# A gated delta-rule scan in chunks: where the matmuls of the values' half and of the u half of the state update stand on TensorE

## What is computed

```python
# H, N = 4, 64 (heads, channels per head); x is (2, 4096, 256), run() goes over all tokens
def step(S, inp):
    rt, dt, kt, vt, at, bt = inp
    sa = jnp.einsum('bhij,bhj->bhi', S, at)
    S = S * dt[:, :, None, :] + sa[..., None] * bt[:, :, None, :] + vt[..., None] * kt[:, :, None, :]
    y = jnp.einsum('bhij,bhj->bhi', S, rt)
    return (S, y)
...
xn = _layernorm(x, axis=-1)
s = _L0_attn_ref(xn, ...)        # token mixing, projections, the scan, group norm, output projection
g = _silu(_L0_ffn_ref(xn, L0_ffn_w_gate, L0_ffn_w_up, L0_ffn_w_down))
x = x + s * g
```

## Time and profile before

| | |
|---|---|
| median of 3 runs | 1603.26 us (1598.4 to 1605.24) |
| the profiled execution | 1603.78 us, of which 1602.3 us lie between its first and last instruction |
| PE busy | 1493.2 us (93%) |
| DVE busy | 1261.4 us (79%) |
| ACT busy | 1073.9 us (67%) |
| POOL busy | 335.8 us (21%) |
| mean granted TensorE clock | 0.982 of full speed |
| chain that ended last | PE 85%, DVE 6%, issue 2%, DMA 2%, ACT 2% |

### The profile page before, as it was taken

How to read it: one execution, slowest core, us unless ns; L and a number is a source line. 1 busy time by engine, 2 the same in 40 slices (tenths; PEclk the granted TensorE clock), 3 DMA queues, 4 the chain that set the end, 5 groups by cost and what they waited for, 6 DMA issues and landing times.

```text
span 1602.3 us, 56437 instructions
## 1 busy us (share of the span) xinstructions
PE 1493.2 (93%) x24384; PEld 1028.5 (64%) x24384; DVE 1261.4 (79%) x2661; ACT 1073.9 (67%) x1889; POOL 335.8 (21%) x362
## 2 busy tenths in 40 slices
PE   3579999999999999899999989999999999999977
PEld 1256767576676767667676666757666675766755
DVE  2788888888888888788887878888888888878623
ACT  3658587585858758576775858768585876858412
POOL 3020301313040131302213030131304013130101
PEclk9799999999999999999999999999999999999979
DMA  4011120301112030110302112030111203011110
GB/s 149 14 21 21 35 47 17 62 19 40 28 35 47 17 62 19 33 34 24 58 16 46 35 21 47 17 62 19 40 36 32 42 17 62 20 40 28 34 34 28
DMA packets 251462, 58.37 MB, mean 36 GB/s; under 512 B 223696, under 2 KB 250704, under 8 KB 251088
## 3 DMA queue, kind: packets, MB, share of 16 engines
q1 hardware_dynamic: 241936, 41.95, 13.8%
q10 hardware_dynamic: 9280, 12.81, 2.2%
HBM read 36.38 MB, written 18.35 MB: 34 GB/s over the span
## 4 chain that ended last, share of the span: by engine, by line
PE 85%; DVE 6%; issue 2%; DMA 2%; ACT 2%; POOL 1%; SPq 1%; ACTq 0%; DVEq 0%; POOLq 0%
PE bank L536 21%; PE chunk L380 15%; PE bank L546 10%; PE bank L511 4%; PE bank L666 3%; PE chunk L644 3%; PE chunk L616 3%; PE chunk L591 3%; PE chunk L600 3%; PE bank L479 2%; PE bank L519 2%; PE bank L485 2%; DMA smalls<-in_x 2%; PE chunk L630 2%; PE bank L380 2%
## 5 line engine op out<-in xcount | busy, mean ns | idle before, releaser
L1327 POOL TENSOR_TENSOR SF<-ST,CT 128x256 f32<-128x256 f32 x128 | 84.1, 657 | 678.3 <-DVE ST L1213 678.3
L536 PE MATMUL bank<-xT,wg 128*128 128x256 f32 x768 | 202.8, 396 | 13.4 <-DVE VU L983 13.4
L536 PE MATMUL bank<-xT,wu 128*128 128x256 f32 x768 | 201.7, 395 | 4.6 <-DVE hT L1173 4.6
L546 PE MATMUL bank<-wd,hT 128*128 128x256 f32 x768 | 177.2, 384 | 0.9 <-DVE hT L1173 0.9
L536 PEld LDWEIGHTS bank<-xT,wg 128*128 128x128 f32 x768 | 139.2, 191 | 58.7 <-DVE VU L983 24.0
L546 PEld LDWEIGHTS bank<-wd,hT 128*128 128x128 f32 x768 | 144.5, 192 | 27.7 <-issue 7.4
L536 PEld LDWEIGHTS bank<-xT,wu 128*128 128x128 f32 x768 | 139.2, 191 | 34.1 <-issue 7.9
L380 PE MATMUL chunk<-KS,W 128*128 128x512 f32 x320 | 151.1, 603 | 2.3 <-ACT gT L721 2.3
L863 ACT ACTIVATE sg<-bank 128x512 f32<-128x512 f32 x96 | 57.2, 595 | 137.3 <-PE bank L536 125.6
L889 ACT ACTIVATE Y<-chunk 32x256 f32<-32x256 f32 x256 | 96.0, 375 | 50.1 <-PE chunk L600 47.3
L380 PE MATMUL chunk<-big,W 128*112 128x512 f32 (+1 forms) x256 | 121.9, 600 | 2.9 <-POOL big L1286 2.6
(11 more groups left out here) (157 smaller groups left out, 3230.1 us busy)
## 6 DMA issues: line engine op xcount, KB each, us to landing
smalls<-in_x SPq DMA_DIRECT2D x32, 256.0 KB, 3.0
Y<-in_x SPq DMA_DIRECT2D x32, 256.0 KB, 3.0
out<-fsil ACTq DMA_DIRECT2D x32, 256.0 KB, 2.2
scrA<-AM SPq DMA_DIRECT2D x64, 64.0 KB, 1.9
hat<-scrB SPq DMA_DIRECT2D x32, 128.0 KB, 3.1
hat<-scrF SPq DMA_DIRECT2D x32, 128.0 KB, 3.3
KE<-scrA SPq DMA_DIRECT2D x64, 32.0 KB, 2.1
scrT<-KE SPq DMA_DIRECT2D x16, 128.0 KB, 1.7
```

Of the source, the lines that this page charges most:

```text
L536: q = pe.matmul(o[:, TT_ * n2:TT_ * n2 + TT_], w[:, h, 128 * (n + n2):128 * (n + n2) + 128], x_now[:, h], start=(h == 0), stop=(h == NH - 1))
L546: q = pe.matmul(o[:, 256 * m:256 * m + 256], hT[:, n, 128 * m:128 * m + 128], wd[:, n, :], start=(n == 0), stop=(n == NF - 1))
L1327: pool.tensor_tensor(SF[:, :, :, :], ST[:, :, :, :], fade[:, c].unsqueeze(3).to_broadcast([128, B, NH, N]), ALU.mult).then_inc(*faded.up)
```

## The change

`banks_of` now puts `PS` into the chunk's own pair of banks. The update of contraction 64 is split by the kind of key: `values_state(c, h)` multiplies the k rows of `KT` by v (contraction 32), and `updates(c, h)` the b rows by u (contraction 32). `values_state` of a chunk is issued one chunk ahead. All functions take one head now, and after the u copies of chunk c PE issues one piece, s{c}: for each head `values(c + 1)` and `outputs(c)` by turns, and then for each head `values_state(c + 1)` and `updates(c)` by turns. *values* and *values_state* read array rows 64b to 64b+31, *outputs* and *updates* rows 64b+32 to 64b+63. Per tile there are 64 more small matmuls written (384 in place of 320). The pieces y{c} and values{c+1} are gone: a chunk has three pieces, state, u and s. PE waits for `y_out` (ACT's take of chunk c - 1) ahead of s{c} for c of 1 to 6, where before it waited ahead of *values*. ACT's `take(c)` waits for the new state (`st_ready`) in place of `y_done`. All nine long strings are laid out anew.

```diff
-ORDER = {"pe": ("NNNFNKOOFNNOKVONNNNKVKRRBKBNNRNNNBBNBBVBNNBVBBNBBEBNBBVBBNBBVBXBBNNBXBBNBBXBXBBNBBNBXBBXNBBLBXBBNXBB"
...
+ORDER = {"pe": ("NNNNFKOOFNNOKVNNNONKRKVRBKBNNVRNNBBNBNBNNBVBEBVBBNBNBVBXBNNBXXBNBNBXBNBNBXBXNBLBXBNXBXLXXXLL"),
...
@@ banks_of
-            z, z_next = chunk_banks[c % 2], chunk_banks[1 - c % 2]
-            return z[:, :, 0:128], z[:, :, 128:256], z_next[:, :, 256:384]
+            z = chunk_banks[c % 2]
+            return z[:, :, 0:128], z[:, :, 128:256], z[:, :, 256:384]
@@ back, on PE
+                def values_state(c, h):
+                    _, _, PS = banks_of(c)
+                    h2, hh = h // 2, 64 * (h % 2)
+                    for b in range(B):
+                        pe.matmul(PS[hh:hh + 64, b, 64 * h2:64 * h2 + 64], KT[par][64 * b:64 * b + 32, c, h2, hh:hh + 64],
+                                  V[64 * b:64 * b + 32, c, 64 * h:64 * h + 64], start=False, stop=False, skip_group_check=True)
+
+                def updates(c, h):
...
+                        q = pe.matmul(PS[hh:hh + 64, b, 64 * h2:64 * h2 + 64], KT[par][64 * b + 32:64 * b + 64, c, h2, hh:hh + 64],
+                                      V[64 * b + 32:64 * b + 64, c, 64 * h:64 * h + 64], start=False, stop=True, skip_group_check=True)
...
-                values(0)
+                for h in range(H):
+                    values(0, h)
+                for h in range(H):
+                    values_state(0, h)
...
-                    if c:
-                        outputs(c - 1)
-                        yield f"y{c - 1}"
...
-                    if c + 1 < QC:
-                        values(c + 1)
-                        yield f"values{c + 1}"
                     pe.wait_ge(*u0_ready(t, c + 1))
                     pe.wait_ge(*u1_ready(t, c + 1))
-                    if c == QC - 1:
+                    if 1 <= c < QC - 1:
                         pe.wait_ge(*y_out(t, c))
                     for h in range(H):
-                        h2, hh = h // 2, 64 * (h % 2)
-                        for b in range(B):
-                            q = pe.matmul(PS[hh:hh + 64, b, 64 * h2:64 * h2 + 64], KT[par][64 * b:64 * b + 64, c, h2, hh:hh + 64],
-                                          V[64 * b:64 * b + 64, c, 64 * h:64 * h + 64], start=(c == QC - 1 and h < 2), stop=True, skip_group_check=True)
+                        if c + 1 < QC:
+                            values(c + 1, h)
+                        q = outputs(c, h)
+                    q.then_inc(*y_done.up)
+                    for h in range(H):
+                        if c + 1 < QC:
+                            values_state(c + 1, h)
+                        q = updates(c, h)
                     q.then_inc(*s_done.up)
                     yield f"s{c}"
-                outputs(QC - 1)
-                yield f"y{QC - 1}"
@@ take, on ACT
-                    act.wait_ge(*y_done(t, c + 1))
+                    act.wait_ge(*st_ready(t, c + 1))
```

More of the change, by code:

```diff
@@ L581, in back, with values @@
                         pe.wait_ge(*taken(t + 1, 1))
-                def values(c):
+                def values(c, h):
                     RY, _, _ = banks_of(c)
[L585 to L588, removed]
-                        for b in range(B):
-                            g = half(h, b)
-                            pe.matmul(RY[g:g + 64, b, 64 * h2:64 * h2 + 64], A[64 * b:64 * b + 32, c, 64 * h:64 * h + 64],
-                                      V[64 * b:64 * b + 32, c, 64 * h:64 * h + 64], start=(h < 2), stop=True, skip_group_check=True)
@@ L594, in outputs @@
-                def outputs(c):
-                    RY, _, _ = banks_of(c)
-                    for h in range(H):
-                        h2 = h // 2
-                        for b in range(B):
-                            g = half(h, b)
-                            q = pe.matmul(RY[g:g + 64, b, 64 * h2:64 * h2 + 64], A[64 * b + 32:64 * b + 64, c, 64 * h:64 * h + 64],
-                                          V[64 * b + 32:64 * b + 64, c, 64 * h:64 * h + 64], start=False, stop=True, skip_group_check=True)
-                    q.then_inc(*y_done.up)
@@ L604, in back @@
-                values(0)
+                    h2 = h // 2
+                    for b in range(B):
+                        g = half(h, b)
+                        pe.matmul(RY[g:g + 64, b, 64 * h2:64 * h2 + 64], A[64 * b:64 * b + 32, c, 64 * h:64 * h + 64],
+                                  V[64 * b:64 * b + 32, c, 64 * h:64 * h + 64], start=(h < 2), stop=True, skip_group_check=True)
+                def values_state(c, h):
+                    _, _, PS = banks_of(c)
+                    h2, hh = h // 2, 64 * (h % 2)
+                    for b in range(B):
+                        pe.matmul(PS[hh:hh + 64, b, 64 * h2:64 * h2 + 64], KT[par][64 * b:64 * b + 32, c, h2, hh:hh + 64],
+                                  V[64 * b:64 * b + 32, c, 64 * h:64 * h + 64], start=False, stop=False, skip_group_check=True)
@@ new lines, in updates, with outputs @@
+                def updates(c, h):
+                    _, _, PS = banks_of(c)
+                    h2, hh = h // 2, 64 * (h % 2)
+                    for b in range(B):
+                        q = pe.matmul(PS[hh:hh + 64, b, 64 * h2:64 * h2 + 64], KT[par][64 * b + 32:64 * b + 64, c, h2, hh:hh + 64],
+                                      V[64 * b + 32:64 * b + 64, c, 64 * h:64 * h + 64], start=False, stop=True, skip_group_check=True)
+                    return q
+                def outputs(c, h):
+                    RY, _, _ = banks_of(c)
+                    h2 = h // 2
+                    for b in range(B):
+                        g = half(h, b)
+                        q = pe.matmul(RY[g:g + 64, b, 64 * h2:64 * h2 + 64], A[64 * b + 32:64 * b + 64, c, 64 * h:64 * h + 64],
+                                      V[64 * b + 32:64 * b + 64, c, 64 * h:64 * h + 64], start=False, stop=True, skip_group_check=True)
+                    return q
```

24 lines of the change are left out of this document (11 added, 13 removed).

## The result

The changed kernel takes **1644.51 us** (median of 4 runs, 1643.04 to 1655.82); the kernel before, run on the same chip, 1601.58 (1598.4 to 1605.24). Ratio of the runs 1.0269, 95% interval 1.0234 to 1.0304. The forecast was 1612 with a range of 1590 to 1630: the sign was right, the size was not, and 1644 lies outside the range. The profiled execution of the changed kernel has a span of 1642.9 us (1644.31 us with what lies around it).

What follows compares the result with a forecast made beforehand. The prediction took PE's work to bound the tiles: 1.2 us less work and 2.1 us more waits per tile, +12 lowered to +9 for slack, giving 1612 us with a range of 1590 to 1630.

Steps and rivals of the forecast that it cites:

- What bounds the kernel: In the fifteen tiles PE's work sets the time; PE is busy 91.6 of 93 us in one tile.
- The s piece of four blocks, 0.70: On PE, each of the pieces s0 to s6 takes 0.70 us, within bounds of 0.63 to 1.56.
- 1.2 us less work per tile: PE's work per tile: small matmuls 1.0 us less, one fewer break into the net's pieces 0.2 less.
- u behind state in chunk 2, 0.57: In chunk 2 u follows state directly, so PE stands 0.57 us per tile; called sure.
- Chunk 4, the load of x, 0.9, and its sum, 0.3: In chunk 4 PE waits 0.9 us while DVE waits for x, and 0.3 for the state sum behind DVE's other work.
- Chunk 0's sum, 0.4, and chunk 3's copy, 0.2: PE waits 0.4 us for chunk 0's sum behind query products, and 0.2 for ACT's u copy in chunk 3.
- So I put the rest at nothing: Outside the listed waits no new PE wait was counted; the first part of a tile keeps its pieces.
- DVE has 14 us of slack in 93, so what it loses to waits it makes up: In a tile, DVE's 14 us of slack makes up its lost time, so it adds no further cost.
- Waits +2.1 a tile, shaved to +9 us in all: New PE waits add 2.1 us per tile (0.6 to 4); the +12 net total was lowered to +9 for slack.
- The last tile 0, +-5: The last tile's changes together come to 0 us, plus or minus 5, as its clock can vary.
- 3, blocks that don't overlap: Rival: the s piece's four blocks don't overlap like the pair; 1622 us at 0.88 per piece, 1690 at 1.56; chance 0.11.
- rival 4: The page's rule that matmuls start and end in program order holds: 3 us less work per tile, 1590 or less; chance 0.02.

Runs made afterwards that it cites:

- e: The changed kernel with VectorE's statistics of x moved behind the keys' third step: 1633.69 us, ratio 1.0206.
- d: The changed kernel with the residual's second add moved behind the flip of the inverse in DVE's string: 1638.88 us, ratio 1.0189.
- a: The changed program under the old order, with only the letters of the gone pieces taken out of TensorE's string: 1641.36 us, ratio 1.0208.
- g: The kernel before with outputs joined with the values, update not split, old order: 1619.03 us, ratio 1.0062.
- k: g with the s pieces of chunks 2 and 3 one filler later: 1614.82 us, ratio 1.007.
- m: g with the changed kernel's strings for the first and the last tile alone: 1605.91 us, ratio 1.0044.
- n: The kernel before with the changed kernel's strings for the first and the last tile alone: 1591.68 us, ratio 0.9964.
- r: The kernel before with only the state update split, its values' half a chunk ahead, old places and strings otherwise: 1618.8 us, ratio 1.0114.
- b: The old program under the new order, y put directly ahead of u and values directly ahead of s: 1642.51 us, ratio 1.0225.
- f: The changed kernel with the s piece's halves swapped, values_state and updates first, both signals at its end: 1640.9 us, ratio 1.0253.
- i: The changed kernel with the two halves of each s piece apart and a filler piece between them: 1702.22 us, ratio 1.0619.

## Why the prediction was wrong, step by step

- *What bounds the kernel*: right. PE's sequence sets the tiles, and 38 of the 43 us are stands of PE.
- *The s piece of four blocks, 0.70*: **the first step that failed.** It measured 0.84, near the bound of 0.88. The words "because all operands stay in one shape" carried the value to the low end; what counts is that the second 32 records start slower. 7 x 0.14 = 1.0 a tile, 15 us. Of the other pieces, the first and the last (0.63) were right, with 0.62; a single block is 0.39 in every trace.
- *1.2 us less work per tile*: 15 x -1.2 = -18 was expected and +4.6 measured, 23 us off. 15 are the s piece's. Of the other 8 the matrix pieces have 3 (busy 86.7 us before, 89.7 in the changed kernel over the fifteen tiles); the rest was not taken apart.
- *u behind state in chunk 2, 0.57*: right. In every tile *u* starts 0.96 behind *state*, as read from the last tile; the profile books 0.50 of it as idle (13 of the 16 times, 7.6 us, of the list above).
- *Chunk 4, the load of x, 0.9, and its sum, 0.3*: the mechanism was right, the size of the first term half of what was taken. Timelines of DVE and then of PE in one tile of the changed kernel:

```profile
454.82 1.40 DVE L954 BATCH_NORM_STATS2 bns<-smalls 128x6 f32<-128x256 f32 x4 [2.35 <-DMA smalls<-in_x]
456.26 0.38 DVE L958 BATCH_NORM_AGGREGATE mv<-bns 128x2 f32<-128x6 f32 x4
...
459.00 0.16 DVE L962 SCALAR_TENSOR_TENSOR nmean<-mv,rstd 128x4 f32<-128x4 f32 x1 [0.81 <-POOL rstd L1276]
459.07 0.76 DVE L1154 TENSOR_TENSOR KE<-KB,EF 128x256 f32<-128x256 f32 x2
459.86 0.73 DVE L1167 COPY_PREDICATED AM<-mask,bank 128x512 f32<-128x512 uint32 x1
460.48 0.41 DVE L1222 TENSOR_TENSOR ST<-SF,chunk 128x256 f32<-128x256 f32 x1
```
```profile
460.94 0.46 PE L629 MATMUL chunk<-ST,hat 64*64 64x64 f32 x16 [0.73 <-DVE ST L1222]
...
463.37 0.92 PE L535 MATMUL bank<-xT,wu 128*128 128x256 f32 x3 [0.90 <-DVE hT L1182]
```

  DVE waits 2.35 for x, as foreseen, and then 0.81 more for POOL's root, which the walk left out; the state sum ends at 460.89 and *state* 5 had stood 0.73 for it. In the thirteen tiles the s piece waits for DVE's copy 5.5 us in 6 times, 0.4 a tile where 0.9 was taken, and *state* 5 for the sum 4.2 in 8, 0.3 as taken. Run e: worth 0.6% of ratio.
- *Chunk 0's sum, 0.4, and chunk 3's copy, 0.2*: wrong; *state* 1 doesn't stand, and no s piece waits for ACT's copy of u.
- *"So I put the rest at nothing"*: **the second step that failed.** The band stands 9.7 us in 13 tiles (run d), the net's up product behind hT 7.9 in 10: 1.35 a tile, 20 us. The band lies in the first part of a tile, which the text had named as a condition; its stand came from one letter of DVE's string outside the recurrence, where I had not read the order. The stand behind hT lies in the recurrence, in chunk 5 (the second line of PE above; 41 to 43 us behind the band in each of the ten tiles). Before, DVE made that product (1173) ahead of the statistics; the new order has it (1182) at 462.63, behind the late sum of chunk 4 and key products, and by the program PE's up matmul waits for the PSUM bank that it empties. All runs with the new VectorE order have this stand (6 to 13 times in thirteen tiles, also with the statistics later, e) and none with the old one (before, a, g, k, m, n, r). "DVE has 14 us of slack in 93, so what it loses to waits it makes up" took the mean of a tile for the slack at this place.
- *Waits +2.1 a tile, shaved to +9 us in all*: stands grew by 38.4 / 15 = 2.6 a tile. The total was nearer than its terms: misses of both signs, so this is luck. The shaving by 3 us for slack was wrong in sign.
- *The last tile 0, +-5*: -2, inside its bounds, but no test of the 0: the mean clock was 0.92 for 0.85, which by itself is worth some 5 us of full speed (0.15 x 67 - 0.08 x 65, an estimate). *Preparation*: the first band starts at 128.1 instead of 129.4.
- *The rivals*: 3, blocks that don't overlap, was the true one for the work, with its own 19 us; the forecast's waits came on top of it, where I had let the waits absorb half. I priced each rival as taking the place of the forecast and not as adding to it. With the measured 0.84 and without the shaving, 1613 + 15 + 3 = 1631; what it would still have lacked is the band and hT. The price of rival 4 was wrong in itself: the rule as told is one of order and does not keep two blocks from overlapping, while 0.78 is two blocks without any overlap; *u* and *values*, which follow each other on the same row groups, take 0.63. For an s piece of 1.56, 1612 + 90 is 1702, or 1657 with half of it absorbed, not 1690.

What **a** and **b** add: either the program or the order is enough for most of the loss. Each alone costs 2.1 to 2.3% and both 2.7%, with intervals of 0.4 to 0.7 either way. The prediction asked what the new order costs with the new program, and had no view of whether the new program was any cheaper in the old order. r and g answer that: they are the prices of the two parts in the old order.

**What stays open.** That the slow second half comes from the supply of instructions is argued from what it depends on (being second, f; gone when apart, i); no record shows the supply, so it is not shown. A count of 32 records alone does not set it: in run r's trace a values block stands directly ahead of the split update (438.91), and the 32 records of the update, 17th to 48th of the run, still start within 0.27 (439.38 to 439.65), behind a pause of 0.2. The matrix pieces' stands for "issue" (4.6 us in r, 6.7 in g, 8.5 in the changed kernel, 12.6 in a, 0.7 before) were seen and not explained; 4 of r's 8 us of new stands are of this kind. In the changed kernel all ten lie inside a piece, behind records of it and where the program has no wait (at 845.56, behind 41 of 64 records), so no other engine's signal ends them. Not explained either are 5 us of PE's work.

## What to carry to other kernels

Before joining small matmuls into one long piece, measure a piece of the same length: blocks that overlap in pairs need not overlap in fours, and a piece that is split and put elsewhere may have been somebody's cover (the values had covered two copies of u). When a reordering comes with a change, read each engine's moved letters outside of the changed stage too: one of them cost 0.8% here, as much as joining did within the intervals. Rivals whose mechanisms are independent are to be added, not chosen between.

## What the runs showed of the hardware

- Of 64 small matmul records in one piece the first 32 start within 0.27 us, the others are spread over 0.38 to 0.39, whichever operands they have (the changed kernel, run f). The Trainium skill ("TensorE: Matmul & The Clock Gate", the table at its head) gives TensorE's queue a depth of 64; a weight load and a matmul for each of 32 records would be just 64, an estimate. The traces agree with that, but none shows the queue.
- Values and outputs by turns and then an update of 64 rows on the same row groups (run g) need 0.42 + 0.40; a block of 16 calls on all four groups 0.41; one of 8 calls 0.39. The call count matters little up to 16, the number of blocks one after the other much.
- One product on DVE, the group norm's, takes 1.43 us by its median and 4.98 at most; PE then stands 2.8. It happened twice in the profiled execution of the kernel before and not in the changed kernel's; why was not tested:

```profile
L1227 DVE TENSOR_TENSOR Y<-Y,st x16: 1224/1430/4975, 197.0 to 1589.6; 128x1024 f32<-128x1024 f32 x16
```
```profile
L1236 DVE TENSOR_TENSOR Y<-Y,st x16: 1226/1430/1636, 198.5 to 1627.0; 128x1024 f32<-128x1024 f32 x16
```

- Executions of one kernel differ with the mean granted clock: of g's ten, the span is 1599.3 at 0.990 and 1622.5 at 0.978.
